# Experts as fp32 64x64 products with combine weights spread through DRAM; routing's masks kept in PSUM

## The reference, cut to what matters

```python
def _moe(tokens, router_w, w1, b1, w2, b2):            # tokens: layernormed, [8192, 64]
    logits = tokens @ router_w.T                        # 8 experts
    rw, re = top_k(softmax(logits), 2); rw = rw / rw.sum(-1)
    combine = zeros((N, 8)).at[arange(N)[:, None], re].set(rw)
    out = tokens
    for e in range(8):
        h = gelu(tokens @ w1[e] + b1[e], approximate=False)
        out = out + combine[:, e:e + 1] * (h @ w2[e] + b2[e])
```

## Time and profile before

| | us |
|---|---|
| median of the three runs | 406.21 |
| the runs | 401.69, 406.21, 406.32 |
| the profiled execution's own time | 406.31 |
| its span (first to last instruction on the core) | 404.5 |
| mean granted PE clock in it | 0.924 of full speed |

### The profile page before, as it was taken

The page is one execution under the profiler, slowest core; times in us unless marked ns, Lnnn a source line. Parts: engine busy times, 40 slices in busy tenths (PEclk is TensorE's granted clock), DMA queues, the critical chain, the costliest instruction groups (busy, mean ns, idle before and its releaser), DMA issues.

```text
span 404.5 us, 7796 instructions
## 1 busy us (share of the span) xinstructions
PE 346.0 (86%) x2889; PEld 215.8 (53%) x2889; DVE 266.4 (66%) x782; ACT 176.2 (44%) x325; POOL 162.0 (40%) x165
## 2 busy tenths in 40 slices
PE   0177788996479999999999999999776999999995
PEld 0167787975354655655655545566453444444442
DVE  6978436458769787687785885996624455565563
ACT  1154324321154554555555644445523445545441
POOL 7965145024746745634320033699910800000000
PEclk9999669757569999999999999999969999999999
DMA  6320000000000000000000000000000000000001
GB/s 214 92 54 2 1 1 2 2 0 0 1 2 0 2 1 2 1 1 2 2 0 1 2 1 3 2 2 2 0 2 0 2 28 28 28 27 27 7 24 52
DMA packets 10345, 6.21 MB, mean 15 GB/s; under 512 B 6104, under 2 KB 10244, under 8 KB 10308
## 3 DMA queue, kind: packets, MB, share of 16 engines
q1 hardware_dynamic: 10308, 5.71, 4.8%
HBM read 3.61 MB, written 2.10 MB: 14 GB/s over the span
## 4 chain that ended last, share of the span: by engine, by line
PE 48%; POOL 24%; issue 14%; DVE 10%; ACT 3%; POOLq 0%; DVEq 0%; ACTq 0%
PE pair L1717 7%; PE pair L1730 7%; PE pair L1705 7%; PE pair L1613 4%; POOL ln_rstd L583 3%; POOL rstd L534 3%; PE pair L1571 3%; PE pair L1419 3%; PE pair L1553 3%; PE pair L1409 3%; POOL hl L559 3%; POOL x L560 2%; POOL rstd L461 2%; POOL xn L522 2%; POOL x L524 2%
## 5 line engine op out<-in xcount | busy, mean ns | idle before, releaser
L1101 DVE SCALAR_TENSOR_TENSOR hid<-pair,neg_shift,YZ 128x512 f32<-128x512 f32 x64 | 45.1, 747 | 39.2 <-PE pair L1717 39.2
L817 DVE TENSOR_TENSOR scaled<-act,pair 128x512 f32<-128x512 f32 x64 | 43.5, 682 | 26.9 <-PE pair L1571 22.6
L1245 ACT ACTIVATE act<-pair,cols 128x512 f32<-128x512 f32 x64 | 43.9, 686 | 36.1 <-PE pair L1553 34.9
L1340 ACT ACTIVATE hid<-pair,bn 128x1024 f32<-128x1024 f32 x32 | 38.5, 1205 | 43.1 <-PE pair L1705 42.9
L1553 PE MATMUL pair<-xs,w1s 128*128 128x512 f32 x128 | 46.6, 446 | 0.0
L583 POOL TENSOR_TENSOR ln_rstd<-ln_var,neg_half 128x8 f32<-128x8 f32 x16 | 26.4, 1658 | 43.5 <-DVE ln_var L837 43.5
L1571 PE MATMUL pair<-scaled,w 128*64 128x256 f32 x256 | 40.7, 398 | 0.0
L1730 PE MATMUL pair<-hid,fo 64*64 64x256 f32 x512 | 33.9, 380 | 0.6 <-DVE hid L1101 0.6
L1705 PE MATMUL pair<-xs_ffn,f1f 64*64 64x512 f32 x256 | 34.4, 609 | 0.0
L1717 PE MATMUL pair<-hid,f 64*64 64x512 f32 x256 | 34.2, 604 | 0.0
L1613 PE MATMUL pair<-xp,vconv 64*64 64x256 f32 x512 | 32.4, 401 | 0.0
(11 more groups left out here) (225 smaller groups left out, 673.8 us busy)
## 6 DMA issues: line engine op xcount, KB each, us to landing
out_dram<-x SPq DMA_DIRECT2D x8, 256.0 KB, 2.5
x<-in_x_dram SPq DMA_DIRECT2D x3, 512.0 KB, 5.9
x<-in_x_dram SPq DMA_DIRECT2D x2, 256.0 KB, 2.9
w1f<-in_L_ffn_w_dram SPq DMA_DIRECT2D x2, 128.0 KB
f1f<-in_L_ffn_W_dram SPq DMA_DIRECT2D x2, 128.0 KB
fo<-in_L_ffn_Wo_dram SPq DMA_DIRECT2D x2, 128.0 KB
w<-in_L_ffn_w_dram SPq DMA_DIRECT2D x2, 64.0 KB
wd<-in_L_conv_Wd_dram SPq DMA_DIRECT2D x2, 64.0 KB, 2.3
```

The costliest lines, as they stand in the source:

```text
L817: v.tensor_tensor(scaled[:, n % 2, :], act[:, n % 2, :], bank[2 + n % 2][:, :], ALU.mult).then_inc(hidden_scaled, 1)
L1101: v.scalar_tensor_tensor(out=hid2[:, n % 2, u, :].rearrange("p (j n) -> p j n", j=2), in0=h, scalar=neg_shift2[:, k, u:u + 1], in1=w, op0= ...
L1245: s.activation(act[:, n % 2, :], bank[n % 2][:, :], ACT.Gelu, bias=cols[:, n % KP:n % KP + 1]).then_inc(hidden_gelu, 1)
L1340: s.activation(hid1[:, n % 2, :, :], pair_of("layer1", n)[:, :, :], ACT.Relu, scale=bn1[:, 0, k:k + 1], bias=bn1[:, 1, k:k + 1]).then_inc( ...
```

## The change

- **Products.** w1s, the high and low halves, hl, sel's use and chl go. `moe_first(b, k)` is eight fp32 matmuls of 64 rows, 64 columns and 256 tokens (2 experts x 2 x 2 tiles), for all 1,024 tokens of the batch, into a whole pair of banks; `moe_second(b, k)` is eight more. So there are four steps k per batch in place of eight n.
- **Gelu and scale.** A gelu runs per expert, in place in PSUM (two of 128x512 per k). `moe_scale` is one product of 128x1024 per k: PSUM times the tile `spread` in SBUF, into SBUF.
- **Combine weights.** `moe_c` is one transpose, ACT copies 64x128 to SBUF (`c_copy`), SP writes it to DRAM (c_dram), waits for that, and reads it back with eight DMAs per batch, each of 4 KB into each of 64 partitions (2.1 MB per batch).
- **Routing.** 16 steps in place of 19, in two parts, placed for batch b + 2 (before: b + 1) between `moe_scale(b, 2)` and `(b, 3)`, and behind `(b, 3)`. Logits, masked logits and three of the masks stay in PSUM (bank 7). `bn_stats` of batch b + 4 are put between the steps.
- **Around it.** Transposes of tokens and of results 4 each (before 8 and 4), logits 4 fp32 matmuls; the bias product is eight matmuls of 128 columns and waits for the copy of the last result (one result buffer in place of two). POOL loses the low part, works one batch further ahead, and clears a larger bias tile at the start. `moe_first(0, 0)` and `(0, 1)` are issued before the gate's second half is there. Eight small bias loads are added.

Core of the diff:

```diff
+            for b in range(NB):
+                sp.wait_ge(c_copied, b + 1)
+                sp.dma_start(c_dram.ap()[b].rearrange("h e (r n) -> (h e r) n", r=T), cT[:, b % 2, :]).then_inc(c_written, 16)
+                sp.wait_ge(c_written, 16 * (b + 1))
+                for k in range(KP):
+                    wait(sp, hidden_scaled, KP * (b - 2) + k + 1)
+                    wait(sp, c_spread[k], 32 * b)
+                    for th in range(2):
+                        sp.dma_start(spread[b % 2][halves(th), 2 * k:2 * k + 2, :, :].rearrange("p e i n -> p (e i n)"),
+                                     rep(c_dram.ap()[b, th, 2 * k:2 * k + 2].rearrange("(a e) n -> a (e n)", a=1), 0, C)).then_inc(c_spread[k], 16)
...
+                    TT(mx(4), mx(1), mx(0), ALU.subtract).then_inc(route_step, 1)
+                    TT(by_e(one2), by_e(tmp), bc(mx(1)), ALU.is_equal).then_inc(route_step, 1)
...
+            def moe_scale(b, k):
+                N = KP * b + k
+                dve.wait_ge(c_spread[k], 32 * (b + 1))
+                dve.wait_ge(hidden_gelu, 2 * N + 2)
                 wait(dve, second_done, N - 1)
-                v.tensor_tensor(scaled[:, n % 2, :], act[:, n % 2, :], bank[2 + n % 2][:, :], ALU.mult).then_inc(hidden_scaled, 1)
+                v.tensor_tensor(scaled[:, N % 2].rearrange("p u i n -> p i u n"),
+                                pair[N % 2][:, :, :].rearrange("p i (u n) -> p i u n", u=2),
+                                spread[b % 2][:, 2 * k:2 * k + 2, :, :].rearrange("p u i n -> p i u n"), ALU.mult).then_inc(hidden_scaled, 1)
...
+            for b in range(NB - 1):
                 moe_scale(b, 0)
                 moe_scale(b, 1)
                 if b == NB - 2:
                     ln_start(0, 0)
+                moe_scale(b, 2)
+                if b:
+                    moe_add(b - 1)
+                if b + 2 < NB:
+                    route(b + 2, 0, b + 4)
+                if b + 4 < NB:
+                    moe_aggr(b + 4)
+                moe_scale(b, 3)
+                if b + 2 < NB:
+                    route(b + 2, 1)
...
+            def gelu(b, k):
+                N = KP * b + k
                 act_e.wait_ge(hidden_done, N + 1)
+                for u in range(2):
+                    h = pair[N % 2][:, :, 2 * P * u:2 * P * (u + 1)]
+                    e = ROW_B1 + 2 * k + u
+                    s.activation(h, h, ACT.Gelu, bias=cols[:, e:e + 1]).then_inc(hidden_gelu, 1)
...
+            for b in range(NB):     # ACT
                 gelu(b, 0)
+                if b == 0:
+                    tanh(1)
+                if b + 2 < NB:
+                    evac_x(b + 2)
+                if b + 1 < NB:
+                    c_copy(b + 1)
...
                 gelu(b, 1)
+                if b:
+                    evac_y(b - 1)
                 gelu(b, 2)
...
                 gelu(b, 3)
+                if b + 2 < NB:
+                    tanh(b + 2)
...
+            def moe_first(b, k):
+                N = KP * b + k
+                wait(pe, hidden_scaled, N - 1)
+                if k == 0:
+                    pe.wait_ge(tok_T_copied, b + 1)
+                for u in range(2):
+                    e = 2 * k + u
+                    for i in range(2):
+                        for th in range(2):
+                            last = t.matmul(pair[N % 2][halves(th), i, 2 * P * u:2 * P * (u + 1)], w1f[halves(i), C * e:C * (e + 1)],
+                                            xs[halves(i), b % 3, 2 * P * th:2 * P * (th + 1)], start=True, stop=True)
+                last.then_inc(hidden_done, 1)
...
             for b in range(NB):     # PE
+                if b:
+                    moe_first(b, 0)
+                    moe_second(b - 1, 2)
+                if b + 2 < NB:
+                    moe_x(b + 2)
+                if b + 1 < NB:
+                    moe_c(b + 1)
+                if b:
+                    moe_first(b, 1)
+                    moe_second(b - 1, 3)
+                moe_first(b, 2)
+                moe_second(b, 0)
+                if b:
+                    moe_back(b - 1)
+                if b + 2 < NB:
+                    moe_logits(b + 2)
+                moe_first(b, 3)
+                moe_second(b, 1)
```

More of the change, by code:

```diff
@@ L805, in moe_add, with step @@
[L805 to L815 removed]
+                def step(n, after):
+                    dve.wait_ge(route_step, base + after)
@@ new lines, in c_copy, with evac_y @@
+            def c_copy(b):
+                act_e.wait_ge(c_T, b + 1)
+                wait(act_e, c_written, 16 * (b - 1))
+                wait(act_e, second_done, KP * (b - 2) + 1)
+                s.activation(cT[:, b % 2, :], bank[7][0:T2 * E, P:2 * P], ACT.Copy, scale=0.5).then_inc(c_copied, 1)
+            def evac_y(b):
+                act_e.wait_ge(second_done, KP * (b + 1))
+                wait(act_e, moe_y_back, b)
+                s.activation(yTs[:, :].rearrange("p (h n) -> p h n", h=2), pair[2][:, :, 0:2 * P], ACT.Copy).then_inc(moe_y_copied, 1)
@@ L1575, in back, with moe_c @@
[L1575 to L1580 removed]
+            def moe_c(b):
+                pe.wait_ge(route_step, 16 * (b + 1))
+                t.transpose(bank[7][0:T2 * E, P:2 * P], cw[:, :], ident[:, :]).then_inc(c_T, 1)
@@ new lines, in moe_bias @@
+            def moe_bias(b):
+                wait(pe, moe_y_copied, b)
+                pe.wait_ge(c_copied, b + 1)
+                for th in (1, 0):
+                    for u in range(2):
+                        for i in range(2):
+                            last = t.matmul(pair[2][halves(i), th, P * u:P * (u + 1)], b2m[:, 4 * th + 2 * i + u, :], cT[:, b % 2, :],
+                                            start=(u == 0), stop=False)
+                    if th:
+                        last.then_inc(bias_in, 1)
@@ new lines, in moe_second @@
+            def moe_second(b, k):
+                N = KP * b + k
+                if k == 0:
+                    moe_bias(b)
+                pe.wait_ge(hidden_scaled, N + 1)
+                for u in range(2):
+                    for th in range(2):
+                        if k == 0 and u == 0 and th:
+                            pe.wait_ge(bias_in, b + 1)
+                        for i in range(2):
+                            last = t.matmul(pair[2][halves(i), th, 0:2 * P], w2[halves(th), 2 * k + u, :], scaled[halves(th), N % 2, u, i, :],
+                                            start=False, stop=(k == KP - 1 and u == 1))
+                last.then_inc(second_done, 1)
```

477 lines of the change are left out of this document (176 added, 301 removed).

## The result

The changed kernel takes 381.5 us (380.3 to 383.6 over four runs), beside 406.3 us for the kernel before; the ratio is 0.943 with an interval of 0.934 to 0.952. The profiled execution has a span of 379.7 us, where the one before had 404.5. It is faster by about 25 us; the forecast was 383.

What follows compares the result with a forecast made beforehand. PE bounds the old kernel, 15.9 of 16.0 us per batch; afterwards waits set 13.1. 131.8 + 3 x 13.1 + 2 x 12.5 = 196.1, plus 24.1 and 0.4: convolution at 220.6, 23.4 saved, 383 us (377 to 390).

Steps and rivals of the forecast that it cites:

- The sum: Whole kernel: convolution starts at 220.6 us where it starts at 244.0 now, 23.4 saved, 383 us in all.
- PE per batch: MoE stage: fp32 products 6.9 us plus transposes, logits, bias and tile-form changes make 10.9 us of PE work per batch.
- DVE per batch: MoE stage: scale 4.9, add 0.7, routing 3.6 and 0.5, aggregation 0.6 make 10.3 us, under today's 12.1.
- a routing step: Routing part 0 on DVE, masks in PSUM: dependent steps 0.28 us apart, bounds 0.26 and 0.36; kernel 381 or 390 at those.
- batch: MoE loop: waits between engines set 13.1 us per batch, 12.5 where nothing is aggregated.
- first scale: Start of the MoE stage: first scale moves from 119.3 to 122.4 us, as DVE does statistics and route(1) first.
- the likeliest case: Whole kernel: the forecast of 377 to 390 us, chance 0.53.
- The step of 0.4 us for the larger clear: Kernel start: POOL's larger clear, 128x512, takes 0.5 us in place of 0.14, 0.4 on the path.
- Rival 1: PE's pause in MoE batches: clock falls to half, +2.8 us for five batches, 397, or every other batch, 390; chance 0.22.
- Rival 2: MoE spread: DMA at 142 GB/s bounds the batch at 14.8 us, +1.7 to 2.3 for six batches, 394; chance 0.08.
- Rival 3: MoE spread: eight transfers one behind the other, 22.5 us per batch with the write, 449 us, slower than before; chance 0.09.
- Rival 4: MoE loop: some eight hand-overs at 0.5 us each in place of 0.1, batch back at 16, 400 to 410; chance 0.08.

## Why the prediction was right, and where it was not

**The sum.** By its own steps, against the traces:

| step | predicted | measured |
|---|---|---|
| PE per batch | 10.9 us | 10.6 |
| eight fp32 products | 0.86 | 0.86 to 0.91 from one start to the next |
| DVE per batch | 10.3 | 9.4 |
| a routing step | 0.28 (0.26 to 0.36) | 0.265 |
| batch | 13.1; 12.5 without aggregation | 12.55; 12.0; two at 13.9 and 13.3 |
| PE's pause | 1.6 | 1.8 |
| first scale | 122.4 | 119.07 |
| first scale to `moe_scale(0, 3)` | 9.4 | 11.1 |
| start of `moe_scale(0, 3)` to that of `(5, 3)` | 64.3 | 64.3 |
| `moe_scale(5, 3)` to the convolution | 24.1 | 23.2 |
| convolution starts | 220.6 | 217.7 |

Of the prediction's own signs, PE is busy 84% of an undisturbed batch (near 85 forecast), the transfers run at 171 GB/s over the seven batches (near 160), one scale waits for a transfer, 0.8 us (none), and the clock is 0.96 in the stage, just above the 0.95 that was to count against it.

**Errors that cancel.** The loop's order was right, hand-over by hand-over: four more routing steps lengthened a batch by 0.9 us, and the transpose moved off the loop shortened it by 0.5. Its length was 0.55 us too long: routing and aggregation take 3.83 us where 4.24 were put (3.6 + 0.64), and the first step starts 8.71 us into the batch, not 8.85. Over five batches that is 2.7 us too much. The two clock drops, which the likeliest case did not hold, are 2.6 us too little. So 64.3 came out as 64.3 by luck; with the pause filled it is 61.6.

**The first scale** was 3.3 us early, and 3.5 of that are the clock between 76 and 90 us, which was half in the trace that the sum was made against and full in the other, on code that the change doesn't touch. The step of 0.4 us for the larger clear was right (0.38). **The opening** gave 1.7 us of it back, which no step of the sum had: the second scale waited 0.81 us for its rows, and PE was at half clock until 123.7, its first products of the batch 1.99 us long in place of 1.09. **Behind the convolution** 1.5 us went the other way, 162.0 us in place of 160.5, as in the second trace of the kernel before. A sum made against one execution carries that execution's clock; here it is a few microseconds of either sign. So the total, 383 for 381.5, is right in its mechanism and better in its number than its parts were.

**Masks in PSUM.** The step in PSUM was taken at 0.28 as the nearest rows had it: right. The port time was told in the right terms and used too little. The prediction charged nothing to it, with one POOL operation, 1.28, as the most it could cost. In the first trace that nearly holds (`mx(4)` takes 0.46 us once and 0.38 once, at the start), in the second it took 1.20 us, in the opening; all are at the start, where POOL is behind, and none is in the batches that the hand-timing was made for. But the prediction never asked what the masks would have cost in SBUF, so the part of the change that they carry stood nowhere. Put back, they cost 7.5 us, beside a gain of 25: held and slower steps, and a clock that falls more often.

**Rival 1, the clock in PE's pause,** at 0.22, was right in its mechanism, and happened, at half its price: two batches and not five, and 1.3 us each, not 2.8, since the clock was back after some 3.3 us, not the 6.5 of the earlier trace rows. "Every other batch: 390" put 7 us on the drops, which cost 2.6. The prediction argued against it from the clock of the old stage, where PE never paused; that evidence did not bear on the new one.

**Rival 2, bound by the spread.** The step that failed is the rate. 281 GB/s was taken; the traces show 230 to 250 while the reads run, about 9 us a batch, and the estimate from the Trainium skill (SBUF — State Buffer, Door 1: The DMA port swizzle), 9.6 us at 218 GB/s, was the closer one. The page calls 218 GB/s the best for 64 partitions, and the measurement is above it (240 and 248 GB/s over 8 us of two batches' reads); the eight reads of a batch go to the lower and the upper 64 partitions in turn, and no run shows what one half would get alone. The transfers were hidden at either rate: the run with hardly any of them took the same time. But reads of 9 us and a write that lands after 2.8 leave under 1 us of a batch of 12.5, where the forecast's 7.5 and 2.5 left 3 of 13.1, and the run with the transpose later used it up: the scale waited for rows in five more batches, and the last lost what the others had gained.

**Rival 3, slower,** would have needed the eight reads one behind the other. They land 5.6 us after their issue, several at once. **Rival 4**: the hand-overs cost what they were put at; DVE's idle 1.64 and 1.39 are the loop itself.

**What stays open.** What decides in which batches the clock falls was not found. Pauses of 1.8 us were followed by a drop in the third and the fourth batch and by none in the second, in the changed kernel twice and in the one without the spread; a pause of 1.87 us in the sixth batch by none; pauses of 1.4 us, with the transpose later, by none; pauses of 2.1 us, with the masks in SBUF, by a drop each time; five pauses of 2.2 to 2.9 us, with the longer routing, by none and a sixth, of 2.77, by one. The transfers are ruled out, and so is the length of the pause alone. The batch's own length differs between these kernels (12.55, 14.13, 13.45 us), and so where the pause falls in time. The Trainium skill (TensorE: Matmul & The Clock Gate, Part 1) says that the gate's watching runs on freely, whatever the kernel does. That would make it matter where a pause falls in time; it does not say why the same two batches were hit in three traces, and no run here tested it.

## What to carry to other kernels

When a cheaper engine turns a full queue into a loop of hand-overs, list three things again: how long each engine's pause is (the clock may fall behind it; idle products put into it cost nothing here), which transfer has the least to spare (the next improvement will stop there), and which short steps share SBUF with POOL. An edit that pulls one wait off the loop, as the transpose later, should be costed with the chain that it delays, here write, landing and read, 10 us long (195.50 to 205.65). And a trace's start may hold some 3 us of clock chance; look twice before explaining them.

## What the runs showed of the hardware

- TensorE went to half clock behind a pause of 1.8 us in a stream that was otherwise dense, and was back after some 3.3 us, at a cost of 1.3 us. In two looks at the same program, and in a third with hardly any transfers, the same two batches were hit. Other pauses, of up to 2.88 us, were followed by no drop.
- 64 partitions that each read the same 4 KB pieces of DRAM got 230 to 250 GB/s from sixteen DMA engines, reads to the lower and the upper half of the partitions in turn; 2.1 MB a batch slowed no compute engine by more than 0.01 us.
- A write of 32 KB lands 1.8 us after its issue when nothing else is under way and up to 6.6 us when it is issued beside 2 MB of reads, from its own queue as well; beside 4.2 MB it took 11.7.
- A VectorE step that reads two tiles of SBUF, 0.26 us alone, takes up to 1.30 us under GpSimd; the same step with one tile in PSUM keeps 0.23.
